# Value product of the self-attention as three float32r passes of split operands, with ACT's order of `out_weights` and `exps` exchanged

## The reference, cut to what matters

```
x = x + attn(layernorm(x), weight_qkv, weight_proj)

qkv    = einsum('sbh,ph->sbp', tokens, weight_qkv)       # 8 groups, each 4 q heads, 1 k, 1 v, of 128
scores = einsum('bhsd,bhtd->bhst', q, k) / sqrt(128)     # causal
attn   = softmax(scores)
out    = einsum('bhst,bhtd->bhsd', attn, v)
result = einsum('sbe,he->sbh', out, weight_proj)
```

## Time and profile before

| | before |
|---|---|
| runs | 3618.52 us median of 3 (3617.93 to 3620.3) |
| profiled execution | 3618.95 us |
| its span in the profile | 3616.8 us |
| granted TensorE clock, mean | 0.977 of 2.4 GHz |
| TensorE busy | 3440.5 us (95%) |
| VectorE busy | 1494.1 us (41%) |
| ACT busy | 1185.0 us (33%) |
| GpSimd busy | 1250.3 us (35%) |
| self-attention part | from the start to about 2030 us |

### The profile page before, as it was taken

The page is one execution under the profiler, slowest core; times in us unless marked ns, Lnnn a source line. Parts: engine busy times, 40 slices in busy tenths (PEclk is TensorE's granted clock), DMA queues, the critical chain, the costliest instruction groups (busy, mean ns, idle before and its releaser), DMA issues. The chain is left out here.

```text
span 3616.8 us, 49438 instructions
## 1 busy us (share of the span) xinstructions
PE 3440.5 (95%) x18100; PEld 2677.0 (74%) x18100; DVE 1494.1 (41%) x2238; ACT 1185.0 (33%) x1679; POOL 1250.3 (35%) x563
## 2 busy tenths in 40 slices
PE   6999999999999999999999679989979999998999
PEld 5888887888878888878787467767767777763587
DVE  3232332323332232423232446656656665652453
ACT  3232232323233232323222235445444454440110
POOL 4334343434324343434342334434334443320000
PEclk9999999999999999999999889999999999999999
DMA  4323233323333232332221254544555455534032
GB/s 168 106 94 113 89 135 130 115 93 106 127 128 117 93 110 93 128 134 89 85 93 53 108 150 128 173 146 137 156 152 137 129 161 162 141 88 157 35 133 76
DMA packets 137253, 431.16 MB, mean 119 GB/s; under 512 B 24112, under 2 KB 24112, under 8 KB 137144
## 3 DMA queue, kind: packets, MB, share of 16 engines
q1 hardware_dynamic: 131384, 408.58, 35.1%
q10 hardware_dynamic: 5760, 20.97, 1.4%
HBM read 316.21 MB, written 37.75 MB: 98 GB/s over the span
## 5 line engine op out<-in xcount | busy, mean ns | idle before, releaser
L446 POOL TENSOR_TENSOR sa_wl<-sa_wraw,sa_wh 128x1024 fp32r<-128x1024 f32 x192 | 458.2, 2402 | 777.3 <-ACT sa_wh L597 777.3
L53 PE MATMUL sa_u<-sa_ln_xh,sa_wh 128*128 128x512 f32 x1536 | 628.5, 409 | 4.4 <-DVE sa_ln_xl L254 4.4
L54 PE MATMUL sa_u<-sa_ln_xl,sa_wh 128*128 128x512 f32 x1536 | 599.7, 390 | 0.0
L55 PE MATMUL sa_u<-sa_ln_xh,sa_wl 128*128 128x512 f32 x1536 | 599.3, 390 | 0.0
L457 POOL TENSOR_TENSOR sa_pl<-sa_praw,sa_ph 128x1024 fp32r<-128x1024 f32 x128 | 318.0, 2516 | 446.4 <-ACT sa_ph L649 446.4
L53 PE MATMUL sa_pr<-sa_ph,sa_oh 128*128 128x512 f32 x1024 | 428.6, 419 | 0.1
L746 DVE TENSOR_TENSOR sa_acc<-sa_pr,sa_acc 128x512 f32<-128x512 f32 x256 | 176.9, 692 | 569.3 <-PE sa_pr L55 569.3
L54 PE MATMUL sa_pr<-sa_pl,sa_oh 128*128 128x512 f32 x1024 | 400.8, 391 | 0.0
L55 PE MATMUL sa_pr<-sa_ph,sa_ol 128*128 128x512 f32 x1024 | 400.0, 391 | 0.0
L738 DVE TENSOR_TENSOR sa_ol<-sa_o,sa_oh 128x512 fp32r<-128x512 f32 x128 | 88.6, 692 | 718.5 <-ACT sa_oh L661 718.5
L53 PEld LDWEIGHTS sa_u<-sa_ln_xh,sa_wh 128*128 128x128 f32 x1536 | 289.3, 188 | 83.6 <-issue 24.2
(11 more groups left out here) (185 smaller groups left out, 5765.7 us busy)
## 6 DMA issues: line engine op xcount, KB each, us to landing
sa_wraw<-in_wqkv SPq DMA_DIRECT2D x192, 512.0 KB, 3.5
sa_praw<-in_wproj SPq DMA_DIRECT2D x128, 512.0 KB, 3.5
ca_wraw<-w_folded SPq DMA_DIRECT2D x96, 512.0 KB, 3.2
ca_kstack<-ca_kmh SPq DMA_DIRECT2D x256, 128.0 KB, 2.4
ca_wraw<-in_wo SPq DMA_DIRECT2D x33, 512.0 KB, 4.2
ca_kstack<-ca_kml SPq DMA_DIRECT2D x128, 128.0 KB, 2.4
ca_qstack<-ca_qh SPq DMA_DIRECT2D x256, 64.0 KB, 2.5
sa_nat<-in_w_nat SPq DMA_DIRECT2D x24, 512.0 KB, 4.7
```

The costliest lines, as they stand in the source:

```text
L53: nc.tensor.matmul(out, ah, bh, start=(first and i == 0), stop=False)
L54: nc.tensor.matmul(out, ah, bl, start=False, stop=False)
L55: ins = nc.tensor.matmul(out, al, bh, start=False, stop=(last and i == len(parts) - 1))
L446: nc.gpsimd.tensor_tensor(wl[:, u % 3], wraw[:, u % 3], f32(wh[:, u % 3]), ALU.subtract).then_inc(w_split, 1)
```

## The change

The value product is made by `three_passes`. For that v is split: ACT writes `vh` (float32r), VectorE the new `low_v`, `vl` = v - `vh`, and `v_copied` is now raised by VectorE. The probabilities are split too: VectorE makes one transpose of all of `probs` into `probsT`; ACT's new `spread_probs` copies it, in four instructions of 32 partitions, to the high part `diagh`; VectorE's new `low_probs` subtracts, again in four instructions, `diagh` from `probsT` into the low part `diagl`. GpSimd clears two tensors instead of one. In ACT's order `out_weights([0, 1])` stands ahead of `exps()`, and `spread_probs()` behind `out_weights([2, 3])`.

```diff
@@ -325,11 +325,14 @@
         kT = sb("sa_kT", [P, 2, BT])
         qT = sb("sa_qT", [P, 2, QPG, BT])
         vT = sb("sa_vT", [P, BT])
-        v = sb("sa_v", [P, 2, TILES, HD])
+        vh = sb("sa_vh", [P, 2, TILES, HD], F32R)
+        vl = sb("sa_vl", [P, 2, TILES, HD], F32R)
         BLK = TILES * QPG
         masked = sb("sa_masked", [P, BLK, QW])
         probs = sb("sa_probs", [P, BLK, QW])
-        diag = sb("sa_diag", [P, BLK, QUADS, QW])
+        probsT = sb("sa_probsT", [P, BLK, QW])
+        diagh = sb("sa_diagh", [P, BLK, QUADS, QW], F32R)
+        diagl = sb("sa_diagl", [P, BLK, QUADS, QW], F32R)
         top = sb("sa_top", [P, BLK])
         total = sb("sa_total", [P, BLK])
         inv = sb("sa_inv", [P, BLK])
...
@@ -438,7 +444,8 @@
         def _(pool):
             pool.sem_inc(w_split, 3)
             pool.sem_inc(p_split, QPG)
-            nc.gpsimd.memset(diag[:], 0.0).then_inc(diag_zeroed, 1)
+            nc.gpsimd.memset(f32(diagh[:]), 0.0).then_inc(diag_zeroed, 1)
+            nc.gpsimd.memset(f32(diagl[:]), 0.0).then_inc(diag_zeroed, 1)
 
             def weights(n, u):
 
@@ -541,8 +548,9 @@
                         pe.wait_ge(diag_ready, m * QUADS + QUADS)
                     pe.wait_ge(o_split, m * TILES + (t + 1))
                     heads = slice(t * QPG, (t + 1) * QPG)
-                    nc.tensor.matmul(o_ps[t % 2][:], v[:, mp, t], diag[:, heads].rearrange("p h q n -> p (h q n)"),
-                                     start=True, stop=True).then_inc(o_done, 1)
+                    three_passes(nc, o_ps[t % 2][:],
+                                 [(vh[:, mp, t], vl[:, mp, t], diagh[:, heads].rearrange("p h q n -> p (h q n)"),
+                                   diagl[:, heads].rearrange("p h q n -> p (h q n)"))]).then_inc(o_done, 1)
 
                 def project(t):
                     if not s.attn:
@@ -622,8 +630,8 @@
                     if not s.proj:
                         return
                     act.wait_ge(v_turned, n + 1)
-                    nc.scalar.activation(v[:, s.par].rearrange("p t d -> p (t d)"), v_ps[:], ACT.Copy
-                                         ).then_inc(v_copied, 1)
+                    nc.scalar.activation(vh[:, s.par].rearrange("p t d -> p (t d)"), v_ps[:], ACT.Copy
+                                         ).then_inc(v_hi, 1)
 
                 def copy_fold(half):
                     if not s.steady:
@@ -654,16 +662,28 @@
                     act.wait_ge(s_shifted, m + 1)
                     nc.scalar.activation(probs[:], probs[:], ACT.Exp, scale=SELF_SCALE).then_inc(exp_done, 1)
 
+                def spread_probs():
+
+                    if not s.attn:
+                        return
+                    act.wait_ge(diag_zeroed, 2)
+                    act.wait_ge(o_done, m * TILES + 1)
+                    act.wait_ge(probs_turned, m + 1)
+                    for q in range(QUADS):
+                        rows = slice(q * QW, (q + 1) * QW)
+                        nc.scalar.activation(diagh[rows, :, q], probsT[rows], ACT.Copy).then_inc(diag_hi, 1)
+
                 def high_o(t):
                     if not s.attn:
                         return
                     act.wait_ge(o_done, m * TILES + (t + 2))
                     nc.scalar.activation(oh[:, t % 2], o_ps[t % 2][:], ACT.Copy).then_inc(o_hi, 1)
 
+                out_weights([0, 1])
                 exps()
-                out_weights([0, 1])
                 copy_unit(0)
                 out_weights([2, 3])
+                spread_probs()
                 copy_unit(1)
                 copy_unit(2)
                 copy_v()
@@ -702,7 +722,16 @@
             def step(s):
                 m = s.m
 
+                def low_v():
+                    if not s.proj:
+                        return
+                    dve.wait_ge(v_hi, s.n + 1)
+                    nc.vector.tensor_tensor(vl[:, s.par].rearrange("p t d -> p (t d)"), v_ps[:],
+                                            f32(vh[:, s.par]).rearrange("p t d -> p (t d)"), ALU.subtract
+                                            ).then_inc(v_copied, 1)
+
                 if not s.attn:
+                    low_v()
                     return
 
                 def softmax():
@@ -727,11 +756,16 @@
                     nc.vector.tensor_tensor(probs[:], probs[:], inv[:].unsqueeze(2).broadcast_to([P, BLK, QW]),
                                             ALU.mult).then_inc(probs_ready, 1)
                     dve.wait_ge(probs_ready, i)
-                    dve.wait_ge(diag_zeroed, 1)
-                    dve.wait_ge(o_done, m * TILES + 1)
+                    nc.vector.transpose(probsT[:].rearrange("p k n -> p (k n)"),
+                                        probs[:].rearrange("p k n -> p (k n)")).then_inc(probs_turned, 1)
+
+                def low_probs():
+                    dve.wait_ge(probs_turned, m + 1)
                     for q in range(QUADS):
                         rows = slice(q * QW, (q + 1) * QW)
-                        nc.vector.transpose(diag[rows, :, q], probs[rows]).then_inc(diag_ready, 1)
+                        dve.wait_ge(diag_hi, m * QUADS + (q + 1))
+                        nc.vector.tensor_tensor(diagl[rows, :, q], probsT[rows], f32(diagh[rows, :, q]), ALU.subtract
+                                                ).then_inc(diag_ready, 1)
 
                 def low_o(t):
                     dve.wait_ge(o_hi, m * TILES + (t + 1))
@@ -750,6 +784,8 @@
                         ln.moments(dve, s.b + 1, [t])
 
                 softmax()
+                low_probs()
+                low_v()
                 low_o(0)
                 next_moments(0)
                 low_o(1)
```

More of the change, by code:

```diff
@@ L357, in self_attention_phase @@
         v_turned = sem("sa_v_turned")
+        v_hi = sem("sa_v_hi")
         v_copied = sem("sa_v_copied")
@@ L367, in self_attention_phase @@
         probs_ready = sem("sa_probs_ready")
+        probs_turned = sem("sa_probs_turned")
+        diag_hi = sem("sa_diag_hi")
         diag_ready = sem("sa_diag_ready")
```

## The result

The changed kernel takes 3720.27 us (median of 4 runs, 3716.16 to 3726.53) against 3618.22 us before on the same chip: a ratio of 1.0284, 95% interval 1.0272 to 1.0296. It is slower by 102 us; 3743 was forecast, 3680 to 3780 the range. The profiled execution took 3716.16 us, with a span of 3714.1.

What follows compares the result with a forecast made beforehand. TensorE was taken as the bound, busy 3440.5 of 3616.8 us. Per step 3.1 wait + 1.6 clock - 0.72 passes = 4.0; 31 x 4.0 + 1 = 124 us, so 3743 us, range 3680 to 3780.

Steps and rivals of the forecast that it cites:

- What delivers late: Self-attention step, VectorE: the four `low_probs` subtractions alternate one by one with GpSimd's instructions, the fourth quarter ready at 339.0 us.
- The gap: TensorE ahead of the value product: waits from 336.0 to 339.1, 3.1 us per step, in 31 of 32 chains.
- The passes: Value product on TensorE: three float32r passes shorten each product by 0.18 us, 0.72 us a step.
- The clock: TensorE after each wait: may run at half its clock, taken as 1.6 us lost per step.
- first rival: Self-attention steps: the gaps come but TensorE's clock stays up, 3694 us; chance 0.14.
- The last step: Last self-attention step, no units to cover the chain: `diag` ready about 2.5 us later, net +1 us (-1 to +3).
- fourth rival: TensorE's clock takes longer to come back, 3.0 us each: +168, 3786 us; chance 0.06 shared with slower passes.
- The clock holds: Self-attention steps: TensorE waits but keeps its full clock, 3694 us; chance 0.14.
- No gap: `low_probs` gets past GpSimd, ready about 4 us before TensorE wants it: 3597 us; chance 0.14.
- One turn less: Two `low_probs` quarters pass between two GpSimd instructions: gap 0.9 us, clock kept, 3626 us; chance 0.06.
- passes no quicker: Value product: float32r passes save 0 instead of 23 us, forecast ends at 3766; chance 0.06 shared with a worse clock.

## Why the prediction was right, point by point

The mechanism is the one forecast, and the time lies in the range of 3680 to 3780, but between two of its cases: below the forecast's own 3725 to 3766 (the text gives 3730 too as its lower end) and above the 3694 of a clock that holds. It fits neither, because the clock fell in half of the steps. That the time is in the range is owed to a range that takes in both cases.

- **What delivers late.** `low_probs` was predicted to take one turn behind each of four GpSimd instructions and to be done 20.8 us behind the last projection (318.2 to 339.0); it was 20.6 us (334.9 to 355.5). The rule of one turn each came from instructions of another kind, TENSOR_SCALAR over 128 x 1024; that it would hold for subtractions on 32 partitions was an inference, and it did. The dose (2.77 us for a quarter) and the second SBUF input (0.69 us without it, 2.42 with it) show the mechanism. L749 was forecast at 0.8 to 1.0 us and L756 below 1.6; they are 0.94 and 1.10 in the median. What was not thought of is the table load that goes with the exponential: in six steps it makes L749 2.22 us, and it costs nothing in the end: `low_probs` still asks in the middle of GpSimd's third, and takes 9.9 us in either kind of step.
- **The gap.** 3.1 us forecast, 2.73 in the trace; from the start that the product would have had it is 2.9 (a step of 63.9 with the clock kept, minus the 60.9 without a gap).
- **The passes.** 0.72 us a step forecast; 0.68 and 0.73 measured. The guess that the changes between float32 and float32r are free held.
- **The clock.** The mis-sized term. 1.6 us is right for one fall (63.88 to 65.5 us), but I had it in all 31 steps and it came in 16 of them, once for twice as long (2.9 us): 26.7 us instead of 50. That the eight gaps of the trace before were all followed by it said less than I took from it: most of them lie among smaller gaps, as the prediction itself says in its first rival.
- **The last step.** Its wait grew by 2.3 us (10.58 to 12.9), about the 2.5 forecast. The net of +1 can't be judged: all that lies behind the last mask grew by 0.1 us, but the same part differs by up to 15 us between kernels that do not change it.
- **The sum.** The 97.3 us between the first mask and the last split into 26.7 of half clock and 70.7 of gap less saving (2.28 a step). These are two parts of one measurement, so that they add up tests nothing; the forecast for them was 50 and 74 (2.38 a step), and the error of the time lies nearly all in the first. In the medians the difference is 102. Within the prediction one sum is off by 1 us: 168 us of the fourth rival added to 3618.95 give 3787, not 3786.
- **The rivals.** "The clock holds" at 3694 is what the kernels with the gap filled show: 3692 and 3684. "No gap" at 3597 is what `probsT` in PSUM shows: 3596. "One turn less" is out, since `low_probs` takes 9.8 to 9.9 us in each of the 31 steps, and so is "passes no quicker", by the 0.68 and 0.73 us.

The changed kernel's 102 us are thus: +91 us of waits for `low_probs` (31 x 2.9), +27 us of half clock behind them, -20 us of passes, and a rest of some 4 us in the medians.

## What to carry to other kernels

Before adding an elementwise instruction to VectorE, count its SBUF inputs and look what GpSimd has queued at that moment: with two, each instruction here cost about a whole one of GpSimd's (2.77 us for the quarter that was left out), so four small ones cost four turns. One large subtraction in their place should cost one, up to the 2.94 us of L727; no run here tries it. An operand that can sit in a free PSUM bank takes the instruction out of the queue, here at no cost that showed. And a wait that TensorE takes in every step can cost more than its length, since the clock may fall behind it; how often is read from the lengths of the steps, not from the mean.

## What the hardware showed that was not expected

- A single stall of 2.7 us brings the clock down in 16 of 31 steps, one of 1.94 us in 14 of 26, one of 1.3 us in none of 31; a fall costs 1.6 us, once 2.9. The same program so has steps of two lengths. These are counts for this place in the step, not a threshold: a stall of 3.06 us left the clock up (620.61, above), and in the cross-attention part of the changed kernel one of 1.46 us (before 2175.0), with three of 0.3 to 0.5 us ahead of it, took the clock from 1.00 to 0.57 over the next four us.
- The scatter of the rest: behind the last mask the part that no kernel here changes took 1609 us (with `probsT` in PSUM) to 1624 us (with 12 matmuls ahead of the product), as measured in one profiled execution each. A difference of a few us between medians of four runs can come from there.
- Idle TensorE can be filled with useless matmuls and the kernel gets faster: 3683.58 against 3720.27 us.
